# TensorE's order in steps 1 to 3 of the last part: the next tile's feed-forward products ahead of the turns

## The chip, the cores and the metric

The kernel runs on one core of a Trainium2 chip. The metric is the device time of one execution in microseconds (us). Five engines work side by side, each through a stream of its own in program order: TensorE (PE, its weight loads shown as PEld), VectorE (DVE), ScalarE (ACT), GpSimd (POOL), and SyncE (SP), which here issues the transfers. They wait for one another on semaphores.

## What is computed

The input is x of 4 x 2048 tokens of width 512, with 128 context keys to each batch. Two layers follow one another:

```python
x = x + L0_xattn(layernorm(x), ctx)          # softmax attention, 16 heads
x = x + L0_ffn(layernorm(x))                 # 8-bit quantised, 512 -> 2048 -> relu -> 512
x = x + L1_xattn(layernorm(x), ctx, mask)    # attention without softmax, then a layer norm of its own
x = x + L1_ffn(layernorm(x))                 # three 512 x 512 products, tanh
```

The quantised feed-forward layer scales its hidden values by their maximum over all tokens. So no token's second product can begin before the first product of every token is done. That splits the kernel.

## The kernel before

The 8192 tokens are 64 tiles of 128 (NT = 64) in 16 groups of four (NG = 16). Four parts follow one another: `prepare` (products of weights), `attend` (the first attention, to 888 us or so), and in `rest` first the products of `w1` for all 16 groups (L1561, to 1142 us), which write the hidden values to DRAM and keep their maximum, and then the last part, which is touched here. Between the two the maximum is brought together across partitions (L1927 to L1932), and the first tiles are rounded.

The last part is a software pipeline over `STEPS = range(-1, NT + 6)`. Each engine has a loop `for k in STEPS` of its own with the order of its work written out by hand; only semaphores tie the loops together. One tile w passes through these stages:

- **ffn2(w)** (PE, L1604 to L1615): the 16 products of the second feed-forward matrix, 128 rows of the rounded hidden values against `w2`. It waits for the rounded values: in the first group (tiles 0 to 3) quarter by quarter (`e_fq`), later for the whole group of four (`e_hq`, so ffn2(4) waits for the fourth of `rounded(4)` to `rounded(7)`), and for `e_x2` of tile w-2, whose PSUM bank it takes.
- **scaled, ffn_out, stats** (DVE, L1832, L1840, L1819 to L1825): scale, add to the residual row X, mean and variance. Then rstd and offset (POOL, L1978, L1984), and **norm** (ACT, L1708) gives the normalised tile xn2(w).
- **turn(w) of xn2** (PE, L1601): four 128 x 128 transposes. **high(w)** (ACT, L1689) copies the transposed tile to `x2Th`, **low(w)** (DVE, L1807) subtracts that from the bank and gives `x2Tl`. **attended(w)** (PE, L1617) makes 12 products of these two with the folded attention matrix `m`.
- **squares(w)** (ACT, L1716), **variance(w)** (DVE, L1873), rstd (POOL), **normed(w)** (DVE, L1882, L1886) and **stats** again give the tile after the second attention; norm (ACT, L1708) gives xn3(w).
- **turn(w) of xn3**, high and low for `x3T`, **last_ffn(w)** (PE, L1630): 12 products with `wc`. Then shifted (DVE), tanh (ACT), result (POOL, L2006), and the store.

In step k TensorE takes turn(k-3) of xn3, turn(k-1) of xn2, ffn2(k+1), attended(k-1), last_ffn(k-3). A tile with a number below 0 is skipped: step -1 is ffn2(0) alone, step 0 ffn2(1) alone, step 1 turn(0), ffn2(2), attended(0), step 2 turn(1), ffn2(3), attended(1); step 3 is the first with all five.

The orders of the others around these steps matter too. DVE takes in step k: low(k-1) for x2T, scaled(k), stats(k-2) of the third norm, low(k-3) for x3T, ffn_out(k), stats(k), in steps 0 and 1 the four `first_round(k+2, q)` (L1787), then `rounded(n)` (L1800) with n = 6, 4 in step 1, 5, 7 in step 2, 8 in step 3, then variance(k-1), shifted(k-4), normed(k-1), flags. ACT takes in steps up to 3: high(k-1), high(k-3), norm(k-2) to xn3, the relu of the hidden values (`hidden`, L1682, n = 6, 4 in step 1, 5, 7 in step 2, 8, 9 in step 3), then norm(k) to xn2 with squares(k-1) behind it (steps 1 and 2) or ahead of it (step 3). SP waits with the load of hidden tile 7 and those behind it (L2050) for `first_round(3, 3)` and its followers.

Of the kernel before, what the change touches and what calls it, by code (L numbers as in the profile page):

```python
# [64 lines left out]
def three(e, out, a, b, first, last):  # L65

    (ah, al), (bh, bl) = a, b
    e.matmul(out, ah, bh, start=first, stop=False)  # L68
    e.matmul(out, ah, bl, start=False, stop=False)  # L69
    return e.matmul(out, al, bh, start=False, stop=last)  # L70
# [13 lines left out]
def cut(i):  # L84
    return slice(i * P, i * P + P)
# [1362 lines left out]
def rest(nc, A, scr, ident, identb, out):  # L1448
# [3 lines left out]
    with ExitStack() as ctx:  # L1452
# [99 lines left out]
        @block.tensor  # L1552
        def _(e):
            def products(u, i):
                if i == 0:
                    e_xT.wait_ge(e, 2 * u + 1)
                e_mx.wait_ge(e, PAIRS * u + i - 3)
                for q in range(2):
                    f = 2 * i + q
                    for k in range(KC):  # L1560
                        last = e.matmul(h_bank[(PAIRS * u + i) % 3][:, q, :], w1[:, k, f * P:f * P + P], xT[u % 2][:, k, :],  # L1561
                                        start=k == 0, stop=k == KC - 1)
                last.then_inc(*e_h)

            def transposes(u, half):
                if u >= NG:
                    return
                e_xn.wait_ge(e, u - 1)
                e_xT.wait_ge(e, 2 * (u - 1) + half)
                for q in range(2):  # L1570
                    for t in range(TPG):
                        last = e.transpose(t_bank[half][:, q, t * P:t * P + P],  # L1572
                                           xn[u % 2][:, t, (2 * half + q) * P:(2 * half + q + 1) * P], identb[:])
                last.then_inc(*e_t)

            def turn_top(e_in, bank, e_done):

                e_in.wait_ge(e, 0)
                e.transpose(bank[:, 0, 0:P], square[:, 0:P], ident[:]).then_inc(*e_done)

            turn_top(e_top, pairs[2], e_all)
            for t in range(TPG):
                e_xn0.wait_ge(e, t)
                for q in range(KC):
                    last = e.transpose(t_bank[q // 2][:, q % 2, cut(t)], xn[0][:, t, cut(q)], identb[:])
                    if t == TPG - 1 and q % 2 == 1:
                        last.then_inc(*e_t)
            for u in range(NG):
                for i in range(PAIRS):
                    products(u, i)  # L1590
                    if i in (3, 5):
                        transposes(u + 1, (i - 3) // 2)
            turn_top(e_top2, pairs[3], e_all2)

            def turn(w, e_in, e_read, src, bank, e_done):
                if not 0 <= w < NT:
                    return
                e_in.wait_ge(e, w)
                e_read.wait_ge(e, w - 1)
                for k in range(KC):  # L1600
                    last = e.transpose(bank[:, cut(k)], src[w % 2][:, cut(k)], ident[:])  # L1601
                last.then_inc(*e_done)

            def ffn2(w):  # L1604
                if not 0 <= w < NT:
                    return
                t, g = w % 4, w // 4
                if g:
                    e_hq.wait_ge(e, 4 * g - 1)
                e_x2.wait_ge(e, w - 2)  # L1610
                for f in range(FC):
                    if g == 0 and f % 4 == 0:
                        e_fq.wait_ge(e, 4 * w + f // 4)
                    last = e.matmul(y_bank[w % 2], hq[g % 2][:, f, cut(t)], w2[:, f, :], start=f == 0, stop=f == FC - 1)  # L1614
                last.then_inc(*e_y)  # L1615

            def attended(w):  # L1617
                if not 0 <= w < NT:
                    return
                B = w // TPB  # L1620
                e_t2l.wait_ge(e, w)
                e_x3.wait_ge(e, w - 2)
                if w % TPB == 0:
                    e_ml.wait_ge(e, KC * B + KC - 1)
                for k in range(KC):
                    last = three(e, a_bank[w % 2], [x[:, k, :] for x in x2T], [x[:, k, :] for x in m[B % 2]], k == 0,
                                 k == KC - 1)
                last.then_inc(*e_a)

            def last_ffn(w):  # L1630
                if not 0 <= w < NT:
                    return
                e_t3l.wait_ge(e, w)
                e_tanh.wait_ge(e, w - 2)
                for k in range(KC):
                    last = three(e, f_bank[w % 2], [x[:, k, :] for x in x3T], [x[:, k, :] for x in wc], k == 0, k == KC - 1)
                last.then_inc(*e_f)

            e_w.wait_ge(e, 10)
            e_unit.wait_ge(e, 0)  # L1640
            for k in STEPS:
                turn(k - 3, e_xn3, e_t3l, xn3, t3_bank, e_t3)
                turn(k - 1, e_xn2, e_t2l, xn2, t2_bank, e_t2)
                ffn2(k + 1)
                attended(k - 1)
                last_ffn(k - 3)

# [558 lines left out]
```

## Time and profile before

| | us |
|---|---|
| median of three runs | 1806.68 |
| lowest and highest of them | 1806.04, 1807.1 |
| the profiled execution, device time | 1805.24 |
| its span (first to last instruction) | 1803.4 |
| mean granted TensorE clock in it | 0.988 of full |

What lies around the span in the profiled execution is 1805.24 - 1803.4 = 1.84 us. Start times in the rows are us from the span's start. A row of a timeline gives start, duration, engine, line, operation, output and inputs, how many instructions are merged, and in brackets how long the engine had been idle and who released it. Ends of TensorE's instructions are modelled: a group of products is drawn some 0.2 us longer than it holds the engine. `f_pair` are the PSUM banks; `f_room` holds, among others, xn2, xn3 and the rounded values of the odd groups.

### The profile page before, as it was taken

Reading aid. Unit: us, or ns where it says so; the run is one execution under the profiler, and the core shown is the slowest. Engines: PE = TensorE matmul, PEld = TensorE weight load, DVE = VectorE, ACT = ScalarE, POOL = GpSimd, SP = SyncE. Lnnn points to the kernel's source line nnn. Section 1 sums busy time; section 2 is a strip of 40 time slices with the busy share of each in tenths; the row PEclk is TensorE's granted clock in tenths of the full one; section 3 lists DMA queues with packets and bytes.
Section 4 is the critical chain, followed back from the end, with each engine's and each line's share of the span. In section 5 each row is a group of like instructions: output and inputs, shape, how many; then the busy total and the mean of one; then the engine's idle time right before and its main releaser. Section 6 shows DMA issues by size and latency. Waiting matters only on the chain.

```text
span 1803.4 us, 29914 instructions
## 1 busy us (share of the span) xinstructions
PE 1739.2 (96%) x9162; PEld 1297.6 (72%) x9162; DVE 1564.4 (87%) x3587; ACT 1203.7 (67%) x3374; POOL 970.8 (54%) x1076
## 2 busy tenths in 40 slices
PE   8998799999999999999799999899999999999997
PEld 7776688888888888888544444467767677776765
DVE  6867799999999999988689888879888988988885
ACT  4675899999999999999443332366555655655543
POOL 2434466666666666666500000257666776766665
PEclk9999999999999999999999999999999999999999
DMA  8766444555465556544389997254455445445311
GB/s 309 222 219 166 113 129 139 157 156 145 142 160 154 145 148 158 148 124 126 103 302 396 403 392 311 83 195 167 153 178 175 167 164 178 170 151 177 119 59 41
DMA packets 153902, 322.08 MB, mean 179 GB/s; under 512 B 47376, under 2 KB 55568, under 8 KB 136080
## 3 DMA queue, kind: packets, MB, share of 16 engines
q1 hardware_dynamic: 153280, 319.38, 54.8%
q8 instruction: 75, 1.23, 0.3%
q10 hardware_dynamic: 464, 0.79, 0.1%
q14 instruction: 83, 0.68, 0.1%
HBM read 163.86 MB, written 105.91 MB: 150 GB/s over the span
## 4 chain that ended last, share of the span: by engine, by line
PE 46%; DVE 1%; issue 1%; ACT 1%; POOL 1%; POOLq 0%; DVEq 0%; ACTq 0%
PE f_pair L1561 12%; PE f_pair L1614 12%; PE f_pair L68 6%; PE f_pair L70 6%; PE f_pair L69 6%; PE f_pair L1601 3%; PE f_pair L1572 1%; ACT f_hf L1682 0%; DVE f_st L1819 0%; POOL f_rs L1978 0%; ACT f_room L1657 0%; POOL f_ring L2006 0%; DVE f_pair L1832 0%; DVE f_x2Tl L1807 0%; POOL f_off L1984 0%
## 5 line engine op out<-in xcount | busy, mean ns | idle before, releaser
L1306 POOL TENSOR_TENSOR a_pr<-a_pr,a_rcp 128x512 f32<-128x512 f32 x256 | 266.4, 1041 | 247.3 <-DVE a_rcp L1148 247.3
L1056 ACT ACTIVATE a_pr<-a_s,a_nmax 128x128 f32<-128x128 f32 x1024 | 343.4, 405 | 28.1 <-DVE a_nmax L1141 25.7
L1561 PE MATMUL f_pair<-f_room,w 128*128 128x512 bf16 x1024 | 228.2, 382 | 0.9 <-ACT f_room L1670 0.9
L1056 ACT ACTIVATION_READ_ACCUMULATOR a_pr<-a_s,a_nmax 128x1 f32 x1024 | 219.7, 215 | 0.0
L1978 POOL TENSOR_TENSOR f_rs<-f_rs,f_half 128x1 f32<-128x1 f32 x128 | 121.2, 947 | 179.9 <-DVE f_rs L1825 179.9
L1779 DVE CUSTOM_DVE_ANT_0 f_hf<-f_pair,nb,sh 128x512 f32<-128x512 f32 x244 | 172.6, 748 | 29.3 <-PE f_pair L1561 27.6
L1561 PEld LDWEIGHTS f_pair<-f_room,w 128*128 128x128 bf16 x1024 | 99.3, 98 | 116.4 <-issue 2.7
L1141 DVE TENSOR_REDUCE a_nmax<-a_s 128x4 f32<-128x512 f32 x256 | 171.9, 671 | 7.3 <-PE a_s L947 7.2
L1156 DVE TENSOR_TENSOR a_pTl<-a_pt,a_pTh 128x512 fp32r<-128x512 f32 x256 | 168.3, 678 | 7.5 <-ACT a_pTh L1068 3.6
L959 PE MATMUL a_pt<-ident,a_pr 128*128 128x128 f32 x1024 | 157.2, 276 | 7.8 <-POOL a_pr L1306 6.0
L1068 ACT ACTIVATE a_pTh<-a_pt 128x512 fp32r<-128x512 f32 x256 | 152.1, 638 | 4.8 <-PE a_pt L959 4.6
L959 PEld LDWEIGHTS a_pt<-ident,a_pr 128*128 128x128 f32 x1024 | 118.0, 140 | 20.6 <-POOL a_pr L1306 10.2
L1614 PE MATMUL f_pair<-w 128*128 128x512 bf16 x512 | 118.2, 385 | 2.1 <-DVE w L1787 2.1
L1971 POOL MEMSET f_room<- 128x1 f32 x2 | 0.1, 98 | 221.0 <-PE f_pair L1572 221.0
L1614 PE MATMUL f_pair<-w,f_room 128*128 128x512 bf16 x512 | 117.8, 384 | 0.0
L1682 ACT ACTIVATE f_hf<-f_hf,f_col 128x2048 f32<-128x2048 f32 x57 | 113.8, 1997 | 0.0
L68 PE MATMUL f_pair<-wch,f_x3Th 128*128 128x512 f32 x256 | 101.3, 396 | 3.1 <-DVE f_x3Tl L1807 3.1
L1009 PE MATMUL a_v<-a_pTh,a_vp 128*128 128x512 f32 x256 | 100.9, 394 | 1.7 <-DVE a_pTl L1156 1.4
L1009 PE MATMUL a_v<-a_pTl,a_vp 128*128 128x512 f32 x256 | 100.6, 393 | 0.0
L70 PE MATMUL f_pair<-wch,f_x3Tl 128*128 128x512 f32 x256 | 100.6, 393 | 0.0
L69 PE MATMUL f_pair<-wcl,f_x3Th 128*128 128x512 f32 x256 | 100.0, 391 | 0.0
L1708 ACT ACTIVATE f_room<-xr,f_off,f_rs 128x512 f32<-128x512 f32 (+1 forms) x64 | 52.1, 815 | 69.1 <-POOL f_off L1984 69.1
(442 smaller groups left out, 5068.4 us busy)
## 6 DMA issues: line engine op xcount, KB each, us to landing
hidden<-f_hf SPq DMA_DIRECT2D x57, 1024.0 KB, 9.0
f_hf<-hidden SPq DMA_DIRECT2D x57, 1024.0 KB, 4.8
xr<-x SPq DMA_DIRECT2D x96, 256.0 KB, 3.2
xb<-x SPq DMA_DIRECT2D x16, 1024.0 KB, 5.4
x<-xr SPq DMA_DIRECT2D x64, 256.0 KB, 2.3
ctxh<-bqreph SPq DMA_DIRECT2D x126, 128.0 KB, 2.4
f_room<-x SPq DMA_DIRECT2D x15, 1024.0 KB, 10.8
ctxh<-bqreph SPq DMA_DIRECT2D x128, 64.0 KB, 2.1
```

What stands on the lines that cost most here:

```text
L68: e.matmul(out, ah, bh, start=first, stop=False)
L69: e.matmul(out, ah, bl, start=False, stop=False)
L70: return e.matmul(out, al, bh, start=False, stop=last)
L959: last = e.transpose(pt_bank[t % 2][:, j * P:j * P + P], pr[:, t, j, :], ident[:])
L1009: last = e.matmul(v_bank[j // 2][:], vp[c][:, j, :], pT[h][:, j, :], start=j % 2 == 0 and h == 0, stop=j % 2 == 1 and h == 1)
L1056: last = e.activation(pr[:, t, j, :], s_bank[t][:, j * P:j * P + P], ACT.Exp, bias=nmax[kk % 2][:, t, j:j + 1], accum_out=sums[t][:, j:j + 1])
L1141: e.tensor_reduce(nmax[kk % 2][:, t, :], s_bank[t][:].rearrange("p (j n) -> p j n", j=4), AX, ALU.max, negate=True).then_inc(*e_max)
L1156: e.tensor_tensor(pT[1][:, :, at], pt_bank[t % 2][:].rearrange("p (j n) -> p j n", j=4), f32(pT[0][:, :, at]), ALU.subtract).then_inc(*e_plo)
L1306: e.tensor_tensor(p, p, rcp[kk % 2][:, t, :].unsqueeze(2).to_broadcast([P, 4, KEYS]), ALU.mult).then_inc(*e_pn)
L1561: last = e.matmul(h_bank[(PAIRS * u + i) % 3][:, q, :], w1[:, k, f * P:f * P + P], xT[u % 2][:, k, :], start=k == 0, stop=k == KC - 1)
L1614: last = e.matmul(y_bank[w % 2], hq[g % 2][:, f, cut(t)], w2[:, f, :], start=f == 0, stop=f == FC - 1)
L1779: last = e.tensor_tensor_reduce(out=hbuf(n)[:, f % 4, :], in0=h_bank[(PAIRS * u + i) % 3][:, q, :], in1=scr["nb1"][:, f:f + 1].to_broadcas ...
```

## The change

TensorE's loop of the last part takes ffn2(k+1) ahead of the two turns in steps 1, 2 and 3. In every other step, and on every other engine, the order is what it was. Nothing is added or removed.

```diff
             for k in STEPS:
+                if 0 < k <= 3:
+                    ffn2(k + 1)
                 turn(k - 3, e_xn3, e_t3l, xn3, t3_bank, e_t3)
                 turn(k - 1, e_xn2, e_t2l, xn2, t2_bank, e_t2)
-                ffn2(k + 1)
+                if not 0 < k <= 3:
+                    ffn2(k + 1)
                 attended(k - 1)
                 last_ffn(k - 3)
```

So step 1 is ffn2(2), turn(0), attended(0); step 2 is ffn2(3), turn(1), attended(1); step 3 is ffn2(4), turn(0) of xn3, turn(2) of xn2, attended(2), last_ffn(0).

## Rows read from the trace of the kernel before

**Rows 1.** The page: busy time of TensorE, its share of the span
```profile
PE 1739.2 (96%) x9162; PEld 1297.6 (72%) x9162; DVE 1564.4 (87%) x3587; ACT 1203.7 (67%) x3374; POOL 970.8 (54%) x1076
```

**Rows 2.** Chain that ended last, by time: start, us, what
```profile
1146.95 6.22 PE f_pair L1614 x16
...
1190.50 0.66 PE f_pair L1601 x4
1191.16 3.45 PE f_pair L1614 x16
...
1210.08 0.87 PE f_pair L1601 x8
...
1771.72 0.89 PE f_pair L1601 x8
```

**Rows 3.** Timeline of TensorE, steps -1 to 3
```profile
1146.95 9.66 PE L1614 MATMUL f_pair<-w 128*128 128x512 bf16 x32 [2.15 <-DVE w L1787]
1158.19 0.66 PE L1601 MATMUL f_pair<-ident,f_room 128*128 128x128 f32 x4 [1.59 <-ACT f_room L1708]
1158.69 3.62 PE L1614 MATMUL f_pair<-w 128*128 128x512 bf16 x16
1161.95 0.58 PE L68 MATMUL f_pair<-f_m0h,f_x2Th 128*128 128x512 f32 x1
...
1166.32 0.66 PE L1601 MATMUL f_pair<-ident,f_room 128*128 128x128 f32 x4 [1.28 <-ACT f_room L1708]
...
1177.83 1.12 PE L1601 MATMUL f_pair<-ident,f_room 128*128 128x128 f32 x4 [3.84 <-ACT f_room L1708]
1178.74 5.70 PE L1614 MATMUL f_pair<-w,f_room 128*128 128x512 bf16 x16
```

**Rows 4.** Timeline of DVE, steps 1 to 3
```profile
1159.68 0.68 DVE L1807 TENSOR_TENSOR f_x2Tl<-f_pair,f_x2Th 128x512 fp32r<-128x512 f32 x1
...
1169.16 0.68 DVE L1807 TENSOR_TENSOR f_x2Tl<-f_pair,f_x2Th 128x512 fp32r<-128x512 f32 x1
...
1177.10 1.23 DVE L1800 TENSOR_SCALAR f_room<-f_hf 128x2048 bf16<-128x2048 f32 x1 [0.66 <-ACT f_hf L1682]
...
1181.26 0.68 DVE L1807 TENSOR_TENSOR f_x2Tl<-f_pair,f_x2Th 128x512 fp32r<-128x512 f32 x1
```

**Rows 5.** Timeline of ACT, steps 1 to 3
```profile
1157.33 0.81 ACT L1708 ACTIVATE f_room<-xr,f_off,f_rs 128x511 f32<-128x511 f32 x1 [1.87 <-POOL f_off L1984]
1158.89 0.60 ACT L1689 ACTIVATE f_x2Th<-f_pair 128x512 fp32r<-128x512 f32 x1 [0.75 <-PE f_pair L1601]
...
1184.57 0.82 ACT L1708 ACTIVATE f_room<-xr,f_off,f_rs 128x512 f32<-128x512 f32 x1 [4.50 <-POOL f_off L1984]
...
1189.65 0.80 ACT L1708 ACTIVATE f_room<-xr,f_off,f_rs 128x511 f32<-128x511 f32 x1
```

**Rows 6.** Timeline of all engines at the end, where TensorE waits behind two turns
```profile
1779.66 1.03 PE L1601 MATMUL f_pair<-ident,f_room 128*128 128x128 f32 x8
...
1780.74 0.60 ACT L1689 ACTIVATE f_x2Th<-f_pair 128x512 fp32r<-128x512 f32 x1 [0.52 <-PE f_pair L1601]
...
1781.37 0.69 DVE L1807 TENSOR_TENSOR f_x2Tl<-f_pair,f_x2Th 128x512 fp32r<-128x512 f32 x1 [0.46 <-ACT f_x2Th L1689]
...
1782.11 0.50 PE L68 MATMUL f_pair<-f_m1h,f_x2Th 128*128 128x512 f32 x1 [1.41 <-DVE f_x2Tl L1807]
```

**Rows 7.** Stretches: busy time (instructions) of PE, PEld, DVE, ACT, POOL; clock, DMA, GB/s
```profile
184.00:186.00 2.00, 0.38 (x3) 0.41 (x3) 1.67 (x5) 2.00 (x7) 0.45 (x1) 1.00 0.87 197
186.00:188.00 2.00, 1.56 (x8) 1.26 (x8) 1.19 (x4) 1.62 (x10) 2.00 (x3) 0.56 0.53 138
188.00:190.00 2.00, 2.00 (x7) 1.58 (x6) 0.91 (x2) 1.67 (x9) 0.82 (x1) 0.58 0.27 67
...
1157.00:1159.00 2.00, 0.81 (x6) 0.68 (x7) 1.93 (x4) 0.93 (x2) 2.00 (x3) 1.00 0.00 0
...
1176.00:1178.00 2.00, 0.17 (x1) 0.17 (x2) 1.34 (x2) 2.00 (x3) 0.00 (x0) 0.53 0.27 47
```

## The prediction

> **What bounds the kernel now.** I read the page first: TensorE is busy for 96% of the span [rows 1]. Then the chain that ended last, to see where in the last part this holds. From 1210.08 to 1771.72 us the chain is TensorE's alone, 57 steps of (1771.72 - 1210.08) / 57 = 9.85 us with no gap [rows 2]. So a delay that is there when step 5 begins is carried to the end whole, and a gain as well. All that counts is when the pipeline reaches that state. I take the turn of xn2(3) in step 4, at 1190.50 us [rows 2], as the mark. Ahead of it TensorE stands idle before three turns: 1.59 us in step 1, 1.28 us in step 2, 3.84 us in step 3 [rows 3], each time for ACT's norm, L1708. The change aims at these gaps. The timelines of DVE and ACT show the way round: turn, high, low, attended, and on DVE low(k-1) stands at the head of its step, so whoever delays a turn delays all that DVE does in that step.
>
> **Step 1.** ffn2(2) needs x2(0) and the rounded quarters of tile 2; xn2(0), which comes later from the same chain on DVE, POOL and ACT, is there at 1157.33 + 0.81 = 1158.14 [rows 5]. So the products can run in the gap. Sixteen of them hold TensorE 3.45 us, drawn as 3.62 [rows 2, 3]. ffn2(1) is drawn to 1146.95 + 9.66 = 1156.61 [rows 3]; take away the 0.17 and ffn2(2) begins at 1156.44 and ends at 1159.89. There turn(0) begins, 1.70 later than its 1158.19. From a turn of four to high is 0.70 us (1158.19 to 1158.89 [rows 3, 5]); from high to low 0.63 and from low to the first product 0.74 [rows 6]. So high(0) is at 1160.59, low(0) at 1161.22, attended(0) at 1161.96, where it was 1161.95. TensorE gains the gap of 1.59 ahead of the turn and has one of about 1.6 behind it: nothing is won, since the 3.26 us of products from 1158.69 to 1161.95 were what hid turn(0)'s way through ACT and DVE. DVE loses: low(0) was at 1159.68 and goes to 1161.22 [rows 4], **+1.54 us**, and scaled(1), whose input is long ready, stands behind it. All that follows on DVE in step 1 moves by 1.54: ffn_out(1), stats(1), with them xn2(1) (TensorE's gap of 1.28 us in step 2 is the wait for it [rows 3], so this chain has no slack), the roundings of tile 3 and of 6 and 4, variance(0) and normed(0).
>
> **Step 2.** ffn2(3) fills the gap of 1.28 us, and turn(1) follows it. low(1) came directly behind normed(0) on DVE (at 1169.16 [rows 4]), which now comes 1.54 later, so at 1170.70; its high is there by then (ffn2(3) from about 1164.9 to 1168.4, high 0.70 on). So low(1) adds nothing to the 1.54, and attended(1) begins at 1171.44, with a gap of some 2.6 us before it. It isn't on the path. On the path is what step 2 makes behind low(1): the third norm's stats(0), xn3(0), the relu of tiles 5 and 7 behind it on ACT, and rounded(7), 1177.10 + 1.23 = 1178.33 [rows 4], which goes to 1179.87. SP's loads of hidden tiles 7 to 10 wait for the roundings of tile 3 and go with them; ACT takes tile 7 later by the same 1.54, so they cost nothing of their own. Nothing else on SP or POOL is passed over, as the change moves only TensorE's instructions.
>
> **Step 3** is the dear one. turn(2) began at 1177.83 and ffn2(4) at 1178.74 [rows 3], which rounded(7) at 1178.33 had just let go. Now the turns stand behind ffn2(4), which waits for rounded(7) at 1179.87, and xn2(2), ready ahead of it, waits with them. TensorE has then been idle for more than 5 us (from about 1174.3), longer than the 3.84 us in which the granted clock went from 1.00 to 0.53, that is, from 2.4 to 1.2 GHz [rows 3, 7]. So ffn2(4) runs slow. Two rows give sixteen products begun after such a gap: 6.22 us, beginning directly at its end [rows 2], and 5.70 us, with a turn ahead of them [rows 3], against 3.62 warm. Less the 0.17, they hold TensorE 6.05 or 5.53 us; I take the middle, 5.8. Then two turns, whose way is 1.08 to high (1779.66 to 1780.74) and 0.63 to low [rows 6]: low(2) at 1179.87 + 5.8 + 1.08 + 0.63 = 1187.4, where it was 1181.26 [rows 4]: **+6.1 us**. Bounds: 3.45 warm gives +3.8, 6.05 gives +6.4; slow to the last product, 16 x 0.43 (twice 3.45 / 16) = 6.9, gives +7.2.
>
> **From there to the mark.** Behind low(2) on DVE stand scaled(3) and the third norm's stats(1); ACT waited 4.50 us for its offset, then came norm at 1184.57, the relu of tiles 8 and 9, squares(2), norm(3) at 1189.65 and the turn at 1190.50 [rows 2, 5]: one chain without slack, 9.24 us from low(2). So the mark moves by 6.1 too. TensorE takes attended(2), last_ffn(0) and turn(1) in the meantime, which by the steady step are 9.85 less the products' 3.45 and one turn's 0.87 / 2, or 6.0 us [rows 2]; begun 0.74 after low(2) they end 6.7 after it, and TensorE stands idle for about 2.5 us before turn(3).
>
> **The second fall of the clock.** Does a gap of 2.5 us lower it? The gap of 1.59 in step 1 left it at 1.00 [rows 3, 7]; in the stretch 184 to 186 TensorE is busy 0.38 of 2 us, and the clock then shows 0.56 and 0.58 in two stretches of 2 us [rows 7], which is (0.44 + 0.42) x 2 / 0.5 = 3.4 us at half speed. 2.5 us lies on the side of the fall, not far from the border. If it falls, 3.4 us at half speed cost half, 1.7, less what of it lies in the gap itself: 1.5 (0 to 1.7). From step 4 on TensorE is the bound, and this is paid in full.
>
> A rule speaks for the change: the Trainium skill, TensorE: Matmul & The Clock Gate, HAM oscillation — how this bites in real kernels, advises ordering the loop so that all the ready work is done before the wait, "so PE stays warm". By that rule gaps and cold stretch shrink; by my reading of the rows the gaps only go behind the turns and grow. It is the first rival below.
>
> **Sum.** 6.1 + 1.5 = 7.6 us. The profiled execution would go from 1805.24 to 1812.8 (span 1811.0). It lay 1.44 under the median of the runs, so against the median: 1806.68 + 7.6 = **1814.3 us**, 0.42% slower. Measurements of this kernel tell about 0.2%, 3.6 us, from no change, so "same" is 1803.1 to 1810.3.
>
> **Rivals.**
> - *The gaps are filled and nothing takes their place* (faster; 4%). The price would be 1.59 + 1.28 = 2.9 us gained, 1803.8, and with the cold stretch of step 3 gone (5.70 - 3.62 = 2.1) 1801.7. It holds if low(0) isn't delayed, that is, if turn(0) begins before about 1158.36 (1159.68 - 0.70 - 0.62). For it speaks that xn2 is the releaser in all three gaps; against it that the products end 1.5 us after that point. That rule of the skill gives this result.
> - *Delayed, but the clock is soon back in ffn2(4)* (about same; 8%). With 3.45 to 4 us for the products the shift is 3.8 to 4.3 less what DVE or ACT make up, and no second fall: 1810.0 to 1811.0.
> - *No second fall* (slower; 38%). The gap of 2.5 us stays under the limit: 1806.68 + 6.1 = 1812.8, between 1811.9 and 1813.9 with the bounds of ffn2(4).
> - *The forecast* (slower; 44%): 1814.3, between 1812.8 and 1815.7.
> - *Worse* (6%): the products of ffn2(4) slow to the end and the turns as well, or the clock falls once more in a later gap: 7.2 + 1.7 = 8.9 and beyond, 1815.6 to 1818.
> - That the change does nothing isn't a case: the orders on TensorE differ in three steps and the waits show it.
>
> **Range.** The two main cases hold 82%; their bounds with a part of the neighbours' give 1811.2 to 1816.0. Chances: faster 0.04, same 0.07, slower 0.89.
>
> **What would show it.** In the profile after: ffn2(2) directly behind ffn2(1) and a gap of about 1.6 us before attended(0), released by DVE L1807; low(0) at 1161.2 and rounded(7) begun at 1178.6; a gap of over 5 us before ffn2(4), then its products over 5.5 us; low(2) near 1187.4; turn(3) near 1196.6 with a gap of 2.5 us and ACT L1708 as its releaser; granted clock under 1.00 behind it or not; 57 steps of 9.85 as before. I am wrong if low(1) or xn2(1) doesn't move with low(0), if ffn2(4) is warm, or if the steps after the mark have gaps that absorb some of it.

## The result

Measured together with runs of the kernel before, the changed kernel takes 1812.43 us (median), the kernel before 1805.80. The medians are 6.6 us apart. The ratio is 1.0032, with an interval of 1.0023 to 1.0041: 5.8 us slower by the ratio, 4 to 7 by its ends. One of the eight runs of the changed kernel took 3008.1 us, at a mean granted clock of 0.585 where the other seven show 0.985 to 0.987, and the ratio leaves it out. The forecast of 1814.3 was 7.6 us above the median shown then, and 1812.43 lies in its range.

In the profiled execution the span is 1810.6 us, against 1803.4. TensorE's busy time is 2.6 us longer, with the same number of instructions (of the page, answers to [rows 1]):

```profile
PE 1741.8 (96%) x9162; PEld 1297.9 (72%) x9162; DVE 1564.6 (86%) x3587; ACT 1203.9 (66%) x3374; POOL 970.8 (54%) x1076
```

**A zero for comparing.** The parts ahead of the last one differ from execution to execution by up to 3 us: the single transpose L1579, which opens the last part, begins between 1144.4 and 1147.4 us in these profiles. So I count from its start. In the kernel before it is

```profile
1144.47 0.33 PE L1579 MATMUL f_pair<-ident,f_room 128*128 128x128 f32 x1 [2.24 <-DVE f_room L1928]
```

and the timeline of TensorE in the changed kernel, steps -1 to 4 (answers to [rows 3]), is

```profile
1144.72 0.33 PE L1579 MATMUL f_pair<-ident,f_room 128*128 128x128 f32 x1 [2.24 <-DVE f_room L1931]
...
1147.20 13.15 PE L1614 MATMUL f_pair<-w 128*128 128x512 bf16 x48 [2.15 <-DVE w L1790]
1160.18 0.60 PE L1601 MATMUL f_pair<-ident,f_room 128*128 128x128 f32 x4
1162.19 0.50 PE L68 MATMUL f_pair<-f_m0h,f_x2Th 128*128 128x512 f32 x1 [1.41 <-DVE f_x2Tl L1810]
...
1165.16 3.61 PE L1614 MATMUL f_pair<-w 128*128 128x512 bf16 x16
1168.61 0.60 PE L1601 MATMUL f_pair<-ident,f_room 128*128 128x128 f32 x4
1171.67 0.50 PE L68 MATMUL f_pair<-f_m0h,f_x2Th 128*128 128x512 f32 x1 [2.46 <-DVE f_x2Tl L1810]
...
1180.17 5.14 PE L1614 MATMUL f_pair<-w,f_room 128*128 128x512 bf16 x16 [4.13 <-DVE f_room L1803]
1185.14 1.04 PE L1601 MATMUL f_pair<-ident,f_room 128*128 128x128 f32 x8
1187.59 0.50 PE L68 MATMUL f_pair<-f_m0h,f_x2Th 128*128 128x512 f32 x1 [1.41 <-DVE f_x2Tl L1810]
...
1196.11 0.66 PE L1601 MATMUL f_pair<-ident,f_room 128*128 128x128 f32 x4 [2.29 <-ACT f_room L1711]
```

All 48 products of ffn2(0) to ffn2(2) now run on end, and the gaps before the turns in steps 1 and 2 are gone. But each has moved behind its turn: 1.41 us before attended(0), 2.46 before attended(1), both released by low (DVE), then 4.13 before ffn2(4), 1.41 before attended(2), 2.29 before turn(3). In line numbers, DVE's and ACT's lines of this kernel lie 3 higher than before.

This zero is good to some 0.4 us. The first products behind it run at a low clock that comes back sooner in one profile than in another (from 1150 to 1152 us it shows 0.63 in step3_only and 0.50 in the kernel before), so that scaled(0), the first work of DVE on a tile and the same in all kernels, begins 8.72 us behind it in the kernel before and 8.36 in step3_only (timelines of DVE, the first row of the kernel before, the second of step3_only):

```profile
1153.19 0.70 DVE L1832 TENSOR_TENSOR f_pair<-f_pair,s 128x512 f32<-128x512 f32 x1 [0.56 <-PE f_pair L1614]
...
1152.81 0.70 DVE L1835 TENSOR_TENSOR f_pair<-f_pair,s 128x512 f32<-128x512 f32 x1 [0.21 <-PE f_pair L1614]
```

The table of the experiments gives this start too.

The chain that ended last (start, us, what) shows the same way of work as the prediction's sum:

```profile
1160.82 0.61 ACT f_x2Th L1692
1161.45 0.69 DVE f_x2Tl L1810
1162.14 0.62 DVE f_pair L1835
...
1178.88 1.24 DVE f_room L1803
1180.17 5.14 PE f_pair L1614 x16
1185.31 0.89 PE f_pair L1601 x8
1186.22 0.60 ACT f_x2Th L1692
1186.85 0.69 DVE f_x2Tl L1810
...
1195.35 0.71 ACT f_room L1711
1196.11 0.66 PE f_pair L1601 x4
```

Counted from L1579, low(0) is at 16.73 us (1161.45 - 1144.72) where it was at 15.21: +1.52. rounded(7) is at 34.16 where it was at 32.63: +1.53. low(2) is at 42.13 where it was at 36.79: +5.34. turn(3) is at 51.39 where it was at 46.03: +5.36. The end is at 665.88 where it was at 658.93: +6.95. The 1.59 us between the last two are the fall of the clock that the prediction calls the second: ffn2(5), drawn 3.62 us in the kernel before, is drawn 5.30 here. Counting all, it is the third of this stretch. The first slows attended(1), the next begins just ahead of ffn2(4), and between them the clock was nearly back (0.96 in the stretch from 1178 us; columns as in [rows 7]):

```profile
1172.00:1174.00 2.00, 2.00 (x8) 1.62 (x7) 1.89 (x7) 0.00 (x0) 0.59 (x2) 0.76 1.04 426
...
1178.00:1180.00 2.00, 0.00 (x0) 0.00 (x0) 1.34 (x2) 2.00 (x4) 0.00 (x0) 0.96 0.29 94
1180.00:1182.00 2.00, 1.83 (x5) 0.72 (x6) 1.25 (x4) 0.12 (x2) 1.54 (x2) 0.50 0.51 119
1182.00:1184.00 2.00, 2.00 (x8) 0.73 (x6) 1.11 (x2) 0.00 (x0) 1.46 (x2) 0.68 0.94 393
...
1196.00:1198.00 2.00, 1.90 (x9) 1.01 (x10) 1.70 (x3) 1.25 (x3) 2.00 (x3) 0.73 0.92 385
1198.00:1200.00 2.00, 2.00 (x6) 0.74 (x5) 2.00 (x4) 1.77 (x2) 0.70 (x1) 0.50 1.04 397
```

### The profile page after: what moved, and what is told of

The parts are those of the page before. It is cut to its first block, busy times and chain, and to the rows that moved or that the text cites. A ratio compares the mean times of both kernels' runs of the same rounds, so it can differ in the third digit from the quotient of the medians.

```text
span 1810.6 us, 29914 instructions
## 1 busy us (share of the span) xinstructions
PE 1741.8 (96%) x9162; PEld 1297.9 (72%) x9162; DVE 1564.6 (86%) x3587; ACT 1203.9 (66%) x3374; POOL 970.8 (54%) x1076
## 4 chain that ended last, share of the span: by engine, by line
PE 47%; DVE 1%; ACT 1%; issue 1%; POOL 1%; POOLq 0%; DVEq 0%; ACTq 0%
PE f_pair L1614 12%; PE f_pair L1561 12%; PE f_pair L68 6%; PE f_pair L70 6%; PE f_pair L69 6%; PE f_pair L1601 3%; PE f_pair L1572 1%; ACT f_hf L1685 0%; POOL f_rs L1981 0%; ACT f_room L1660 0%; DVE f_x2Tl L1810 0%; DVE f_st L1822 0%; POOL f_ring L2009 0%; POOL f_off L1987 0%; ACT f_x2Th L1692 0%
```

## The experiments

Ten kernels beside the change, each timed against the kernel before. "Turn(3)" and "end" are of the profile, from the start of L1579, against the kernel before (46.03 and 658.93 us); the start of L1579 and the span are given with them, so the end is span less start, less 658.93. "scaled(0)" is its start from that of L1579, 8.72 in the kernel before; what it differs from 8.72 was there ahead of every reordered step, and the text takes it off where it matters. The ratio is of the timed runs.

| kernel | L1579 at | scaled(0) | span | turn(3) | end | median us | ratio, interval |
|---|---|---|---|---|---|---|---|
| the change | 1144.72 | 8.76 | 1810.6 | +5.36 | +6.95 | 1812.43 | 1.0032, 1.0023 to 1.0041 |
| step1_only | 1145.96 | 8.80 | 1806.4 | +1.58 | +1.51 | 1808.03 | 1.0011, 1.0002 to 1.0020 |
| step2_only | 1145.80 | 8.77 | 1805.2 | +0.54 | +0.47 | 1806.56 | 1.0006, 0.9997 to 1.0015 |
| step3_only | 1144.45 | 8.36 | 1808.9 | +4.00 | +5.52 | 1812.19 | 1.0038, 1.0026 to 1.0051 |
| warm_after | 1144.92 | 8.68 | 1807.6 | +3.77 | +3.75 | 1809.43 | 1.0021, 1.0011 to 1.0031 |
| after_warm4 | 1147.26 | 8.46 | 1811.1 | +4.91 | +4.91 | 1812.92 | 1.0034, 1.0022 to 1.0047 |
| split | 1145.08 | 8.69 | 1804.0 | -0.01 | -0.01 | 1806.07 | 0.9998, 0.9989 to 1.0007 |
| step1_low_later | 1144.71 | 8.73 | 1803.6 | -0.11 | -0.04 | 1807.24 | 1.0000, 0.9991 to 1.0009 |
| warm_before | 1146.34 | 8.09 | 1804.6 | -0.62 | -0.67 | 1807.49 | 1.0007, 0.9998 to 1.0016 |
| early_relu | 1146.52 | 8.65 | 1804.4 | -0.9 | -1.05 | 1803.86 | 0.9987, 0.9978 to 0.9996 |
| early_relu_warm | 1147.43 | 8.09 | 1802.8 | -3.50 | -3.56 | 1803.71 | 0.9985, 0.9976 to 0.9994 |

The medians of the kernel before that stand beside them were 1805.87 (the steps alone and warm_after), 1806.42 (split, step1_low_later, warm_before, early_relu) and 1806.83 (after_warm4, early_relu_warm). The timed runs tell some 2 us; differences below that rest on one profile each.

### One step at a time: step1_only, step2_only, step3_only

Each has the change's condition for one step alone, here for step 1:

```diff
+                if k == 1:
+                    ffn2(k + 1)
                 turn(k - 3, e_xn3, e_t3l, xn3, t3_bank, e_t3)
                 turn(k - 1, e_xn2, e_t2l, xn2, t2_bank, e_t2)
-                ffn2(k + 1)
+                if not (k == 1):
+                    ffn2(k + 1)
```

> The order is changed in step 1 alone: ffn2(2) ahead of turn(0). Theory A (a turn behind the products holds up DVE, whose low(0) stands ahead of scaled(1); steps 1 to 3 are bound by the chain through DVE, POOL and ACT, and the gaps of TensorE before its turns are slack): low(0) 1.5 us later, the gap of 1.59 us before turn(0) gone and one of about 1.4 before attended(0) in its place, turn(2) and turn(3) 1.5 us later, the end 1.5 us later (1.2 to 1.8). Rival B (TensorE's idle time in steps 1 to 3 is what the time consists of; only the clock costs): 0 to 1.6 us faster. Rival C (the cost of the change is nearly all of step 3): 0.

> The order is changed in step 2 alone: ffn2(3) ahead of turn(1). Theory A: turn(1) goes from 1166.3 to about 1168.4, low(1) from 1169.16, where it stood behind normed(0), to about 1169.8: only the 0.6 us by which the turn overtakes that cover are passed on, so the end is 0.6 us later (0.4 to 1.0), though TensorE's own turn is 2.1 later. Rival B: 0 to 1.3 us faster. Rival D (every delay of a turn is passed on whole): 2.1 us later.

> The order is changed in step 3 alone: ffn2(4) ahead of both turns. Theory A: rounded(7) stays at 1178.3 and ffn2(4) begins there, with the clock at half speed after a gap of over 4 us, and holds TensorE 4.9 to 6 us; then turns, high and low: low(2) 4 to 4.8 us later than 1181.3, turn(3) in step 4 as much later, with a gap of over 2 us before it. With or without a second fall of the clock behind that gap the end is 4 to 6.3 us later. So step 3 is the largest part of the 6.6, and the three steps alone add up to about the whole. Rival C (all of it is step 3): 6.6.

Step 1 alone costs 1.51 us by the profile. TensorE's gap before attended(0) is 1.41, and turn(1) waits 2.87 us for an xn2(1) that comes late:

```profile
1163.47 0.50 PE L68 MATMUL f_pair<-f_m0h,f_x2Th 128*128 128x512 f32 x1 [1.41 <-DVE f_x2Tl L1810]
...
1169.38 0.66 PE L1601 MATMUL f_pair<-ident,f_room 128*128 128x128 f32 x4 [2.87 <-ACT f_room L1711]
```

Step 2 alone costs 0.47, not the 2.1 us by which its turn is late: low(1) only overtakes normed(0) by a little, and DVE stands idle before it for just 0.40 us:

```profile
1171.02 0.69 DVE L1810 TENSOR_TENSOR f_x2Tl<-f_pair,f_x2Th 128x512 fp32r<-128x512 f32 x1 [0.40 <-ACT f_x2Th L1692]
```

Step 3 alone costs 5.52: 4.00 up to turn(3), and 1.52 behind it for a second fall of the clock as in the whole change. DVE waits 4.26 us before low(2), with scaled(3) and stats(1) behind it (one of the 16 products has no record here):

```profile
1178.41 5.27 PE L1614 MATMUL f_pair<-w,f_room 128*128 128x512 bf16 x15 [5.59 <-DVE f_room L1803]
...
1185.23 0.69 DVE L1810 TENSOR_TENSOR f_x2Tl<-f_pair,f_x2Th 128x512 fp32r<-128x512 f32 x1 [4.26 <-ACT f_x2Th L1692]
...
1194.48 0.66 PE L1601 MATMUL f_pair<-ident,f_room 128*128 128x128 f32 x4 [2.25 <-ACT f_room L1711]
```

1.51 + 5.52 = 7.03, and the whole is 6.95, but that close a match is partly luck: counted from scaled(0) it is 1.43 + 5.88 = 7.31 against 6.91. The difference of 0.40 is no more than the cold products of ffn2(4) differ by: from the end of rounded(7) to the turns it is 5.57 us in step3_only (1177.96 to 1183.53) and 5.03 in the change. So steps 1 and 3 make up the whole to within the spread of the clock, and step 2 is covered once step 1 has delayed DVE. That idle time of TensorE is what counts (rival B) is out for steps 1 and 3; for step 2 alone it is out by the profile, while the timed runs (0.9997 to 1.0015) leave room for it. That it is all step 3 (rival C) is not what the profiles show; the timed runs of step1_only speak against it too, if barely (interval from 1.0002), while by those of step3_only alone it could stand.

### The clock taken away, the waits left: warm_after, after_warm4

```diff
+            def filler(n, bank):
+                for i in range(n):
+                    e.matmul(bank, w2[:, i % FC, 0:P], w2[:, i % FC, :], start=True, stop=True)
...
             for k in STEPS:
+                if k == 3:
+                    filler(23, f_bank[1])
                 if 0 < k <= 3:
                     ffn2(k + 1)
                 turn(k - 3, e_xn3, e_t3l, xn3, t3_bank, e_t3)
+                if k == 4:
+                    filler(9, f_bank[1])
                 turn(k - 1, e_xn2, e_t2l, xn2, t2_bank, e_t2)
                 if not 0 < k <= 3:
                     ffn2(k + 1)
+                if k == 2:
+                    filler(10, f_bank[1])
                 attended(k - 1)
```

after_warm4 has only the 9 of step 4.

> The changed kernel with idle products of w2 with itself (they go to a bank that is free, their result isn't used) in the gaps of TensorE: 10 before attended(1), 23 before ffn2(4), 9 before turn(3). They leave out nothing. They take the cold clock away and leave every wait. Theory A: the clock stays at 1.00 through steps 2 to 4, ffn2(4) holds TensorE 3.5 us in place of some 5, low(2) comes 1.5 to 2.3 us earlier than in the changed kernel, and the cold stretch of step 4 (up to 1.7 us) is gone: the end 2 to 4 us earlier than in the changed kernel, that is about 3.8 us later than before. Rival E (the clock is the whole cost): as fast as before. Rival F (the clock costs nothing, waits are all): no change, 6.6 later than before.

> The changed kernel with 9 idle products of w2 with itself before turn(3) in step 4 and nowhere else; nothing is left out. Theory A (the gap of 2.29 us before turn(3) lets the clock fall, and since TensorE is the bound from there on, its 3.4 us at half speed are paid in full): no fall behind step 4, turn(3) where it was, the end 1.4 to 1.7 us earlier than in the changed kernel. Rival H (that cold stretch is given back later, since the other engines are ahead): no change against the changed kernel.

The timeline of TensorE in warm_after:

```profile
1174.88 4.91 PE L1641 MATMUL f_pair<-w 128*128 128x512 bf16 x22
...
1180.30 3.63 PE L1614 MATMUL f_pair<-w,f_room 128*128 128x512 bf16 x16 [0.50 <-DVE f_room L1813]
...
1194.72 0.66 PE L1601 MATMUL f_pair<-ident,f_room 128*128 128x128 f32 x4 [0.34 <-ACT f_room L1721]
```

ffn2(4) begins where it did (35.38 from L1579, against 35.45 in the changed kernel) and takes 3.63 us, not 5.14; turn(3) comes 1.59 us earlier, and the end 3.20. So of 6.95 us the cold clock is 3.20 and the waits are 3.75, where the sum's floor for a warm clock was 3.8. Neither rival, all clock or all waits, holds by the profile. The timed runs say the same coarsely: the medians are 3.6 us above the kernel before, against 6.6 for the change. They rule out that the clock is all. Against the waits being all they say little, since the intervals (1.0011 to 1.0031, and 1.0023 to 1.0041) overlap.

after_warm4 shows turn(3) and the end later by the same 4.91: nothing is lost behind the turn, where the changed kernel lost 1.59. The end comes 2.04 us earlier than in the changed kernel, more than the 1.4 to 1.7 expected: 1.59 is the loss behind the turn, and the other 0.45 was there at turn(3) already, 0.30 of it at scaled(0) and 0.15 from ffn2(4), drawn 4.99 us in place of 5.14. The timed runs (1.0034) can't tell it from the change. That the fall costs 1.6 us is seen in the profiles of three kernels (the change, step3_only, and its absence here), not in the medians.

### Are the gaps before the turns worth filling? split

```diff
-            def ffn2(w):
+            def ffn2(w, first=0, end=FC):
...
-                for f in range(FC):
+                for f in range(first, end):
...
-                last.then_inc(*e_y)
+                if end == FC:
+                    last.then_inc(*e_y)
...
+                ahead = {1: 7, 2: 5}.get(k, 0)
+                if ahead:
+                    ffn2(k + 1, 0, ahead)
                 turn(k - 3, e_xn3, e_t3l, xn3, t3_bank, e_t3)
                 turn(k - 1, e_xn2, e_t2l, xn2, t2_bank, e_t2)
-                ffn2(k + 1)
+                ffn2(k + 1, ahead)
```

> Only as many products go ahead of the turn as fit in its gap: 7 of ffn2(2)'s 16 in step 1, 5 of ffn2(3)'s in step 2, none in step 3. Theory A (the gaps before the turns are slack, since the path in steps 1 to 3 is the chain through DVE, POOL and ACT, and TensorE's own idle time isn't on it): turn(0) stays where it was, the gaps of 1.59 and 1.28 us go, equally long ones appear before attended(0) or the next turn, end within 0.3 us of before. Rival B (idle time of TensorE is time lost): up to 2.9 us faster.

TensorE's timeline:

```profile
1147.56 11.14 PE L1614 MATMUL f_pair<-w 128*128 128x512 bf16 x39 [2.15 <-DVE w L1791]
1158.77 0.66 PE L1601 MATMUL f_pair<-ident,f_room 128*128 128x128 f32 x4
1159.27 2.11 PE L1614 MATMUL f_pair<-w 128*128 128x512 bf16 x9
```

The gap of step 1 is filled to the full and turn(0) is at 13.69 us from L1579, where it was at 13.72. The end doesn't move (-0.01; ratio 0.9998, 0.9989 to 1.0007). So filling these gaps, with no turn delayed, had nothing to win in steps 1 and 2: TensorE's idle time there is slack of the chain through DVE, POOL and ACT.

### Is it DVE's order? step1_low_later

step1_only, with DVE's low(0) behind stats(1):

```diff
-                low(k - 1, t2_bank, x2T, e_t2h, e_t2l)
+                if k != 1:
+                    low(k - 1, t2_bank, x2T, e_t2h, e_t2l)
                 scaled(k)
...
                 stats(k, st2, mv2, rs2, e_x2, e_bn2, e_ag2, e_xn2, e_ve2)
+                if k == 1:
+                    low(k - 1, t2_bank, x2T, e_t2h, e_t2l)
```

> The order is changed in step 1 alone, as in step1_only, and DVE takes low(0) behind scaled(1), ffn_out(1) and stats(1) in place of ahead of them. Theory A (step 1's cost is DVE standing before low(0) with ready work behind it): xn2(1) and all behind it are where they were before, or 0.7 us later at most where low(0) is now in the way of the roundings; rounded(7) and the end 0.6 to 0.8 us later than before, against 1.5 for step1_only. attended(0) begins about 1 us later than in step1_only, which costs nothing. Rival G (the cost comes from attended(0) or the turn being late, not from DVE's order): 1.5 us or more, growing with attended(0).

The 1.51 us are gone (-0.04), though attended(0) begins later still, behind a gap of 2.47 us. So the cost of step 1 is DVE standing before low(0), not the late turn or the late attended(0). I had expected 0.6 to 0.8 to stay, for low(0) now ahead of the roundings. It didn't, because POOL's offset for xn2(1) came out shorter. In the kernel before it stood beside DVE's rounding of 2048 columns, and norm(1) came behind it (timelines of POOL and ACT):

```profile
1164.04 1.38 POOL L1984 TENSOR_SCALAR f_off<-f_mv,f_rs 128x1 f32<-128x1 f32 x1
...
1165.46 0.81 ACT L1708 ACTIVATE f_room<-xr,f_off,f_rs 128x511 f32<-128x511 f32 x1 [2.19 <-POOL f_off L1984]
```

and here, with low(0) between, most of it was done before that rounding (1164.41 on):

```profile
1163.29 0.58 POOL L1990 TENSOR_SCALAR f_off<-f_mv,f_rs 128x1 f32<-128x1 f32 x1
...
1165.06 0.80 ACT L1711 ACTIVATE f_room<-xr,f_off,f_rs 128x511 f32<-128x511 f32 x1
```

norm(1) is at 20.35 us from L1579 and was at 20.99: the 0.64 won pays for low(0). Had POOL taken as long as before, some 0.6 us would have stayed by this count, as expected, and still not step 1's 1.51.

### The same filling where it should be worth nothing: warm_before

```diff
+                if k == -1:
+                    filler(8, f_bank[1])
                 turn(k - 3, e_xn3, e_t3l, xn3, t3_bank, e_t3)
+                if k in (3, 4):
+                    filler({3: 16, 4: 7}[k], f_bank[1])
                 turn(k - 1, e_xn2, e_t2l, xn2, t2_bank, e_t2)
                 ffn2(k + 1)
```

> The kernel before with idle products of w2 with itself in TensorE's gaps: 8 ahead of ffn2(0), 16 ahead of turn(2) in step 3, 7 ahead of turn(3) in step 4. Nothing is left out. The same means that gave back 3 us in the changed kernel. Theory A: in step 3 ffn2(4) gets 2 us shorter, attended(2) comes up to 2 us earlier, and turn(3) stays where it is, since DVE and ACT bring xn2(3) no earlier: end within 0.5 us of before, with a gap of some 2 us before turn(3), of which the idle products take 1.5. Rival E (a microsecond of cold clock is half a microsecond of time wherever it lies): 2 us faster.

Timelines of TensorE and ACT:

```profile
1158.55 0.81 ACT L1716 ACTIVATE f_room<-xr,f_off,f_rs 128x511 f32<-128x511 f32 x1 [1.22 <-POOL f_off L1992]
...
1179.62 3.63 PE L1614 MATMUL f_pair<-w,f_room 128*128 128x512 bf16 x16
...
1191.75 0.66 PE L1601 MATMUL f_pair<-ident,f_room 128*128 128x128 f32 x4 [0.77 <-ACT f_room L1716]
```

ffn2(4) takes 3.63 us in place of 5.70 [rows 3], 2.07 less, and turn(3) comes 0.62 earlier. That much is there from the first filling already: scaled(0) is 0.63 earlier, and norm(0) is at 12.21 us from L1579 and was at 12.86 (1157.33 [rows 5]). Counted from scaled(0) the end moves by 0.04 us. The median isn't lower at all. Beyond the bound expected by 0.2, but far from rival E's 2 us. The same cold stretch of ffn2(4) is worth 1.6 us in the changed kernel and nothing that can be read in the one before, since there turn(2) and its low had gone ahead of it.

### A version faster than both: early_relu, early_relu_warm

If the chain through DVE, POOL and ACT is the path, then ACT's idle time before norm(k-2) to xn3 is the place to work on: 4.50 us in step 3 [rows 5].

```diff
+                early = {2: (5, 7), 3: (8, 9)}.get(k, ())
+                for n in early:
+                    hidden(n)
                 norm(k - 2, mv3, rs3, off3, xn3, D, e_off3, e_t3, e_xn3)

                 if k <= 3:
                     for n in quarters(k, 1):
-                        hidden(n)
+                        if n not in early:
+                            hidden(n)
```

> TensorE's order is that of before. ACT takes the relu of hidden tiles 5 and 7 (step 2) and 8 and 9 (step 3) ahead of norm(k-2) to xn3, for whose offset it stood idle 4.9 and 4.5 us, and not behind it. Theory A (the path in steps 1 to 3 is the chain through DVE, POOL and ACT, not TensorE): norm(2) to xn2 comes about 2.8 us earlier, turn(2) at about 1175 in place of 1177.8 and with a warm clock, low(2) 2.5 us earlier, turn(3) 4 to 5 us earlier than 1190.5, bound then by TensorE's last_ffn(0): the end 4 to 5 us earlier (at least 2). Rival B (TensorE is the bound in steps 1 to 3 as well, as its share of 96% says): no change.

Faster, but by 1.05 us in the profile (2.3 by the ratio, 0.7 to 4), not 4 to 5, and less than the 2 us that were expected at the least. Two things took the rest, to be read in the timelines of POOL, of DVE and of TensorE of this kernel:

```profile
1175.28 2.22 POOL L1982 TENSOR_TENSOR f_rs<-f_rs,f_half 128x1 f32<-128x1 f32 x1 [0.84 <-DVE f_rs L1829]
1177.60 0.27 POOL L1988 TENSOR_SCALAR f_off<-f_mv,f_rs 128x1 f32<-128x1 f32 x1
```

```profile
1175.11 1.22 DVE L1804 TENSOR_SCALAR f_room<-f_ring 128x2048 bf16<-128x2048 f32 x1
1176.24 1.22 DVE L1804 TENSOR_SCALAR f_room<-f_hf 128x2048 bf16<-128x2048 f32 x1
```

```profile
1178.76 1.11 PE L1601 MATMUL f_pair<-ident,f_room 128*128 128x128 f32 x4 [2.77 <-ACT f_room L1708]
1179.67 6.19 PE L1614 MATMUL f_pair<-w,f_room 128*128 128x512 bf16 x16
```

First, DVE's two roundings now come directly behind stats(2), and POOL's rstd beside them takes 2.22 us in place of 0.55 (which its neighbours of the same form take), so that norm(2) is 1.1 us earlier, not 2.8. Second, ffn2(4) runs cold for 6.19 us, and with the other engines ahead it is TensorE's own chain from it that sets turn(3). The second is a claim that the filling can test:

```diff
+                if k == -1:
+                    filler(8, f_bank[1])
                 turn(k - 3, e_xn3, e_t3l, xn3, t3_bank, e_t3)
+                if k == 3:
+                    filler(10, f_bank[1])
                 turn(k - 1, e_xn2, e_t2l, xn2, t2_bank, e_t2)
```

> TensorE's order of before, the relu of tiles 5, 7, 8 and 9 early as in early_relu, and idle products in two gaps: 8 ahead of ffn2(0), 10 ahead of turn(2) in step 3. In early_relu ffn2(4) ran cold (6.2 us) and TensorE's chain from it set turn(3). Theory A: with DVE and ACT ahead the cold stretch is now on the path, so that the filling that did nothing for the kernel before (or 0.7 us) brings 2 us here: turn(3) 2 us earlier than in early_relu, end 3 to 3.7 us earlier than in the kernel before. Rival: the filling brings as little as in warm_before (under 1 us).

TensorE's timeline:

```profile
1179.58 3.62 PE L1614 MATMUL f_pair<-w,f_room 128*128 128x512 bf16 x16
```

ffn2(4) takes 3.62, and the end is 3.56 us earlier than before in the profile, 2.5 earlier than in early_relu. Of these 2.5 us 0.56 are at scaled(0), from the filling ahead of ffn2(0); the other 1.95 are what theory A gave to the cold ffn2(4) (2 us). The timed runs give 0.9985 (0.9976 to 0.9994), that is 2.7 us with 1 to 4 as its bounds; they show it faster than both kernels, but not how much the filling adds to early_relu (0.9987).

## Why the prediction was right

**Step 1, +1.54.** Measured +1.52 at low(0) and +1.53 at rounded(7); step1_only gives it by itself, and step1_low_later shows that its place is low(0) in DVE's order.

**Step 2, nothing.** The chain of waits goes from normed(0) to low(1) as forecast. The gap before attended(1) was to be 2.6 and is 2.46. What I missed is that I put the question of a falling clock only to the gap in step 4: this one was already followed by a fall (0.76 in the stretch from 1172 us). It slowed attended(1), which therefore ended later and left a gap of 4.13 us, not of over 5. It cost nothing, for attended(1) isn't on the path.

**Step 3** holds the term with the largest error. The form was right (ffn2(4) cold, from rounded(7); then turns, high, low), the size was not. The term of ffn2(4) was 5.8 us, the middle of two rows, and measured 5.14 drawn, or 4.97 held: 0.8 too much. The clock came back sooner than in either of the two rows. The kernel before shows

```profile
1182.00:1184.00 2.00, 2.00 (x8) 0.79 (x7) 1.92 (x6) 0.00 (x0) 0.38 (x1) 0.76 0.53 205
```

and 0.50 in the two stretches ahead of it. Counted as the prediction does, half speed lasts there until about 1183.0, 4.2 us behind the start of ffn2(4); in the changed kernel, with 0.68 in the same stretch, until about 1183.3, but ffn2(4) begins later and that is 3.1 us behind its start.

All the others fit: from the turns' start to high 1.08 us, as in [rows 6]; to low 0.63, measured 0.63. So the shift at low(2) was +5.34, not +6.1. The bound for a warm clock, 3.8, was met by warm_after: +3.75 at low(2), +3.77 at turn(3).

**From low(2) to turn(3)**, 9.24 us without slack: measured 1196.11 - 1186.85 = 9.26. The gap before turn(3), forecast at 2.5, is 2.29.

**The second fall**, +1.5: 1.59 in the change, 1.52 in step3_only, and none where the gap was filled. I had given this case 44% and the case without it 38%, and only the profile tells them apart: 1812.43 lies in the band of the case without the fall (1811.9 to 1813.9) and just under the band of the forecast (1812.8 to 1815.7).

**The number.** Of the 1.9 us between 1814.3 and 1812.43, 0.9 are in the kernel before, whose median was 1805.80 with these runs and 1806.68 when the forecast was made. The profile gives 6.95 us for the 7.6 of the sum, and the products of ffn2(4) are the difference. That the range still reached low enough owes something to luck: 1811.9, from which the case without a second fall begins, is 5.2 us above 1806.68 and stands for products of about 4.9 us, which neither of the two rows gave.

**Nothing given back behind it.** In the nine kernels without a fall behind turn(3) the end moves with turn(3) to within 0.15 us. In the other two it moves 1.59 and 1.52 us further, and ffn2(5) is drawn 1.68 us longer in the change.

**The first rival**, gaps filled and nothing in their place, with the skill's rule at its side, is answered by split and warm_before. The Trainium skill (TensorE: Matmul & The Clock Gate, HAM oscillation — how this bites in real kernels) advises, for matmuls in short bursts between DMA waits, doing all the products of one tile before the wait, "so PE stays warm". The trace doesn't agree for this kernel: with ready products ahead of the waits the gaps went behind the turns, and the clock fell behind the gaps of 2.46 and 2.29 us too, where in the kernel before, from step 1 on, it fell only in that of 3.84. Idle products did keep it up, and what that is worth depends on who is on the path: counted from scaled(0) nothing in the kernel before (0.04 us), 3.12 us in the changed one.

## What to carry to other kernels

- A gap before an instruction is only a loss if its engine is on the path there. A share of 96% over the whole didn't say so for these 45 us; filling two of the gaps moved nothing, while moving whole products into them laid bare the turn's way through two other engines, which the products had covered.
- In streams with a hand-written order, look for who stands at the head of its step waiting for the moved piece, and what ready work is queued behind it. Here it was one subtraction on DVE, and it passed on 1.5 us in step 1, 0.5 in step 2 where it was queued anyway, and 4.0 to 4.4 in step 3, the cold products ahead of the turn included.
- Price a gap also by what the clock does behind it, and ask whether the cold stretch is on the path.

## What the runs showed of the hardware

**Length alone doesn't tell whether a gap lowers the clock.** Gaps of 2.29 (the change) and 2.25 us (step3_only) before turn(3) were followed by a fall, and so was one of 2.46 before attended(1) in the change. The gap of 2.87 before turn(1) in step1_only was not, by these stretches of that kernel:

```profile
1168.00:1170.00 2.00, 0.61 (x5) 0.58 (x6) 1.73 (x3) 1.39 (x3) 0.48 (x1) 1.00 0.77 229
1170.00:1172.00 2.00, 2.00 (x11) 0.88 (x9) 1.30 (x3) 0.60 (x1) 1.77 (x3) 1.00 1.05 438
```

The gap of 2.42 us before turn(0) in warm_before wasn't either: ffn2(2) behind it is drawn 3.62 us, as in the kernel before. What went before the gap differs from case to case, and which part of it decides no run here shows.

Sixteen products begun cold in step 3 took from 4.99 (after_warm4) over 5.14 to 5.70 and 6.19 us (and in step1_only the fifteen that have a record 4.68). A forecast of such a term should keep that whole width.

**DVE's wide roundings stop POOL.** An operation of POOL on one column took 2.22 us beside two of them, 0.55 with none beside it; another 1.38 beside one, 0.27 otherwise. The same is seen later in the kernel before, step after step: at 1207.19 us rstd takes 1.46 us beside the rounding drawn from 1207.02 to 1208.24. The Trainium skill, SBUF — State Buffer, section SBUF: two separate sides, says of the port pair that the two engines share that it is an exclusive lock held for a whole instruction, if DVE's instruction is of a kind that takes both ports. The trace agrees in that POOL never ends before the rounding: the 2.22 us end at 1177.50, the second rounding at 1177.46; the 1.38 us end at 1165.42, the rounding at 1165.38. In which mode the roundings run no run here shows.
